# Row maxima of a first attention layer from 32-row products of two heads in two row groups, and four instead of five key tiles summed on GpSimd

## The reference

```python
tokens = x.reshape(B, C, N).transpose(0, 2, 1)
qkv = (tokens @ w_proj + b_proj).reshape(B, N, NUM_HEADS, 3 * HEAD_DIM)
q, k, v = jnp.split(qkv, 3, axis=-1)
attn = jnp.einsum('bihd,bjhd->bijh', q, k) * SCALE
attn = jax.nn.softmax(attn, axis=2)
res = jnp.einsum('bijh,bjhd->bihd', attn, v).reshape(B, N, NUM_HEADS * HEAD_DIM)
out = res @ w_out + b_out + tokens
```

## Time and profile before

| | |
|---|---|
| median of 3 runs | 2839.39 us |
| profiled execution | 2838.16 us |
| its span, first to last instruction | 2836.4 us |
| TensorE matmul busy | 2652.5 us, 94% |
| VectorE busy | 1983.4 us, 70% |
| ScalarE busy | 1286.8 us, 45% |
| GpSimd busy | 698.3 us, 25% |
| granted TensorE clock, mean | 0.981 |

### The profile page before, as it was taken

The page is one execution under the profiler, slowest core; times in us unless marked ns, Lnnn a source line. Parts: engine busy times, 40 slices in busy tenths (PEclk is TensorE's granted clock), DMA queues, the critical chain, the costliest instruction groups (busy, mean ns, idle before and its releaser), DMA issues.

```text
span 2836.4 us, 44487 instructions
## 1 busy us (share of the span) xinstructions
PE 2652.5 (94%) x15932; PEld 1852.8 (65%) x15932; DVE 1983.4 (70%) x2297; ACT 1286.8 (45%) x1874; POOL 698.3 (25%) x444
## 2 busy tenths in 40 slices
PE   5899999999999999999999999999999999999994
PEld 4457775577656776567755777557775577656772
DVE  2665777666976768766786677766787666876666
ACT  2463435533365434644346343563435534364334
POOL 0440025300372014600236002540035300361011
PEclk7899999999999999999999999999999999999997
DMA  5300023000410005000050002300032000500016
GB/s 127 71 1 16 12 65 77 17 1 12 105 38 17 1 12 112 31 17 1 30 124 2 17 12 51 91 12 5 12 73 69 17 1 12 112 31 1 1 62 275
DMA packets 46238, 123.51 MB, mean 44 GB/s; under 512 B 9905, under 2 KB 21425, under 8 KB 42417
## 3 DMA queue, kind: packets, MB, share of 16 engines
q1 hardware_dynamic: 46000, 120.36, 15.9%
HBM read 41.96 MB, written 23.86 MB: 23 GB/s over the span
## 4 chain that ended last, share of the span: by engine, by line
PE 71%; issue 9%; DVE 6%; ACT 4%; SPq 4%; POOL 3%; DMA 2%; DVEq 0%; ACTq 0%; POOLq 0%
PE tile L1542 21%; PE pv L1542 11%; PE pv L1666 8%; PE tile L1628 7%; PE tile L1656 6%; PE tile L1801 4%; PE tile L1692 4%; SPq L582 3%; PE pv L1656 2%; PE tile L1823 2%; PE tile L1852 2%; DMA stack<-qk_r 1%; ACT p L854 1%; POOL qk_r L687 1%; PE tile L1720 1%
## 5 line engine op out<-in xcount | busy, mean ns | idle before, releaser
L1123 DVE TENSOR_REDUCE small<-tile 128x1 f32<-128x1024 f32 x512 | 600.0, 1216 | 130.8 <-PE tile L1628 128.2
L854 ACT ACTIVATE p<-tile 128x512 f32<-128x512 f32 (+1 forms) x632 | 405.2, 692 | 239.2 <-PE tile L1656 214.4
L745 POOL TENSOR_TENSOR row_sum<-act 128x256 f32<-128x256 f32 x32 | 41.6, 1318 | 1475.8 <-DVE act L1316 1475.8
L1542 PE MATMUL tile<-qk_r 128*128 128x512 f32 x1536 | 378.0, 395 | 0.0
L1628 PE MATMUL tile<-stack 96*128 96x512 f32 x1024 | 344.7, 436 | 19.9 <-DMA stack<-qk_r 14.9
L715 POOL TENSOR_TENSOR acc<-acc,p 128x1024 f32<-128x1024 f32 x144 | 339.2, 2385 | 4.1 <-ACT p L854 3.9
L1542 PEld LDWEIGHTS tile<-qk_r 128*128 128x128 f32 x1536 | 287.4, 188 | 66.2 <-issue 7.7
L1321 DVE TENSOR_TENSOR pl<-p,ph 128x1024 fp32r<-128x1024 f32 x128 | 158.2, 1236 | 220.8 <-ACT p L936 220.8
L1628 PEld LDWEIGHTS tile<-stack 96*128 96x128 f32 x1024 | 178.7, 192 | 188.3 <-issue 118.9
L1656 PE MATMUL tile<-stack 112*128 112x512 f32 x760 | 269.6, 420 | 24.9 <-ACT p L854 18.4
L1666 PE MATMUL pv<-p,v 128*32 128x512 f32 x2048 | 273.1, 610 | 1.4 <-ACT p L854 1.4
(11 more groups left out here) (286 smaller groups left out, 4507.2 us busy)
## 6 DMA issues: line engine op xcount, KB each, us to landing
stack<-qk_r SPq DMA_DIRECT2D x192, 256.0 KB, 5.0
x_in<-in_x_dram SPq DMA_DIRECT2D x8, 1024.0 KB, 5.0
act<-in_x_dram SPq DMA_DIRECT2D x8, 1024.0 KB, 4.9
x_scratch<-act SPq DMA_DIRECT2D x7, 1024.0 KB, 4.0
z_scratch<-act SPq DMA_DIRECT2D x7, 1024.0 KB, 3.9
stack<-ones SPq DMA_DIRECT2D x16, 256.0 KB, 4.7
w3f<-w3f_scratch SPq DMA_DIRECT2D x8, 512.0 KB, 3.3
fin_rest<-z_scratch SPq DMA_DIRECT2D x3, 1024.0 KB, 8.5
```

What stands on the lines that cost most here:

```text
L854: sc.activation(p0[:, jt % DEPTH, pair, first:first + len(heads) * HALF], tile_wait(batch, "st0", *u, jt, k), ACT.Exp, scale=float(D) ** - ...
L1123: ve.tensor_reduce(maxima[:, h * NT + it:h * NT + it + 1], t, X, ALU.max).then_inc(vector_done, vector.one("max0", g, h, it))
L1542: ins = mm(out, lhs[a][kt_], rhs[c][kt_], start=first and kt_ == 0 and m == 0, stop=last and kt_ == n - 1 and m == 2)
```

## The change

- `s0(g, h, it)` is for a pair of heads and one half of the keys: of h, `h // 2` is the pair and `h % 2` the half. Its two matmuls contract over 32 rows, the high parts alone, and lie in the two row groups of the two heads. The second head's result goes to the second bank. In the head (the first unit) they read `qk_r`, elsewhere `stack`. The number of matmuls and of s0 stays.
- `max0` reduces the tile to two maxima, one a head; the two halves of the keys go to `maxima` and `maxima2`, and `max_both` takes the larger.
- The parts of each head are stacked in another order (`ROWS`), so that the product of the high parts of head h lies in row group h. Head 3 has its maxima in rows 64 to 96 (32 rows, of which the first 16 are zeroed by `mask8`), and its st0 contracts over 128 rows.
- VectorE spreads the maxima of heads 0 and 3, ScalarE those of 1 and 2. `key_ones` is two DMAs a group. `neg_copy` and `mh` are gone; `neg_hi` writes to its place at once.
- In the head the s0 wait for no DMA; the first unit's st0 of key tile 0 wait for the stacks.
- SUMMED is 4 in place of 5: in units 0, 1 and 2 GpSimd sums key tiles 0 to 3, den0 takes 4 to 7.

```diff
-K0 = IMAX + NMAX
+ROWS = ((0, 1, 2), (1, 0, 2), (2, 0, 1), (3, 0, 1))
+IMAX_OF = (96, 96, 96, 64)
+NMAX_OF = (NMAX, NMAX, NMAX, 2 * NMAX)
+K0_OF = (IMAX + NMAX, IMAX + NMAX, IMAX + NMAX, P)
+VECTOR_ROWS = (0, 3)
+SCALAR_ROWS = slice(1, 3)
-SUMMED = 5
+SUMMED = 4
...
             def key_ones(g):
-                sp.dma_start(stack[IMAX:K0, g, 1].rearrange("p h (a n) -> p (h a) n", n=P).bitcast(F32),
-                             ones[0:NMAX, :].rearrange("p (a n) -> p a n", a=1)
-                             .broadcast_to((NMAX, G * N // P, P))).then_inc(key_ones_in[g], 16)
+                for rows, n, heads in ((IMAX_OF[0], NMAX_OF[0], slice(0, G - 1)), (IMAX_OF[-1], NMAX_OF[-1], slice(G - 1, G))):
+                    k = heads.stop - heads.start
+                    sp.dma_start(stack[rows:rows + n, g, 1, heads].rearrange("p h (a n) -> p (h a) n", n=P).bitcast(F32),
+                                 ones[0:n, :].rearrange("p (a n) -> p a n", a=1)
+                                 .broadcast_to((n, k * N // P, P))).then_inc(key_ones_in[g], 16)
...
-                    for k, pair in enumerate((slice(0, 4, 2), slice(0, 4, 3), slice(1, 3))):
+                    for k, pair in zip(ROWS[h], (slice(0, 4, 2), slice(0, 4, 3), slice(1, 3))):
...
                 def max0(g, h, it):
                     t = tile_wait("s0", g, h, it)
-                    ve.tensor_reduce(maxima[:, h * NT + it:h * NT + it + 1], t, X, ALU.max
+                    pair, part = divmod(h, 2)
+                    dst = (maxima, maxima2)[part].rearrange("p (h t) -> p h t", h=G)[:, 2 * pair:2 * pair + 2, it]
+                    ve.tensor_reduce(dst, t.rearrange("p (q n) -> p q n", q=2), X, ALU.max
...
+                    if heads == G:
+                        m2 = maxima2.rearrange("p (h t) -> p h t", h=heads)[:, :, ts]
+                        TT(m3, m3, m2, ALU.max).then_inc(vector_done, vector.one("max_both", *key))
+                        own("max_both", *key)
...
                 def s0(g, h, it):
-                    if it == 0 or it == HT:
-                        pe.wait_ge(stacked[g][h], 48 * batch_of(("s0", g, h, it)) + 48)
+                    pair, part = divmod(h, 2)
+                    ahead = of_head(("s0", g, h, it))
+                    if ahead and (h, it) == (0, 0):
+                        scalar_wait("qk0_hi", 1, 0)
+                    elif not ahead and it % HT == 0 and part == 0:
+                        for q in range(2):
+                            pe.wait_ge(stacked[g][2 * pair + q], 48 * batch + 48)
                     o = free("s0", g, h, it)
-                    for s in halves:
-                        ins = mm(o[:, s], stack[0:IMAX, g, 0, h, it * P:(it + 1) * P], stack[0:IMAX, g, 1, h, s],
-                                 start=True, stop=True)
+                    for q in range(2):
+                        rows = slice(D * (2 * pair + q), D * (2 * pair + q) + D)
+                        i = slice(it * P, (it + 1) * P)
+                        queries, keys = ((qk_r[rows, g, t, 0, n] for t, n in ((0, i), (1, halves[part]))) if ahead else
+                                         (stack[rows, g, t, 2 * pair + q, n] for t, n in ((0, i), (1, halves[part]))))
+                        ins = mm(o[:, halves[q]], queries, keys, start=True, stop=True)
...
                 def st0(g, half, jt, k):
...
+                    if (g, half) == UNITS[0] and jt == 0:
+                        for h in heads:
+                            pe.wait_ge(stacked[g][h], 48 * batch + 48)
...
-                        ins = mm(o[:, halves[q]], stack[0:K0, g, 1, h, jt * P:(jt + 1) * P],
-                                 stack[0:K0, g, 0, h, halves[half]], start=True, stop=True)
+                        ins = mm(o[:, halves[q]], stack[0:K0_OF[h], g, 1, h, jt * P:(jt + 1) * P],
+                                 stack[0:K0_OF[h], g, 0, h, halves[half]], start=True, stop=True)
```

More of the change, by code:

```diff
@@ L182, in front @@
         s += [("max", layer, it) for it in range(NT)]
-        s += [("neg_hi", layer), ("neg_copy", layer), ("neg_lo", layer), ("max_in", layer), ("v_lo", layer, 1)]
+        s += [("neg_hi", layer), ("neg_lo", layer), ("max_in", layer), ("v_lo", layer, 1)]
         return s
@@ L208, in vector_steps @@
         s += [("max0", *rows_of(UNITS[0], k))]
-    s += [(n, *UNITS[0]) for n in ("neg_hi", "neg_copy", "neg_lo")]
-    s += [("max_rows", *UNITS[0], h) for h in range(G // 2)]
+    s += [(n, *UNITS[0]) for n in ("max_both", "neg_hi", "neg_lo")]
+    s += [("max_rows", *UNITS[0], h) for h in VECTOR_ROWS]
     for u in UNITS:
@@ L221, in vector_steps @@
         if following:
-            s += [(n, *following) for n in ("neg_hi", "neg_copy", "neg_lo")]
-            s += [("max_rows", *following, h) for h in range(G // 2)]
+            s += [(n, *following) for n in ("max_both", "neg_hi", "neg_lo")]
+            s += [("max_rows", *following, h) for h in VECTOR_ROWS]
     s += [("stat", 1, 0, ct) for ct in range(CT)]
@@ L245, in of_head @@
         return name[1] == 0 and name[3] < HT
-    if kind in ("m0", "neg_hi", "neg_copy", "neg_lo", "max_rows", "max_cols"):
+    if kind in ("m0", "max_both", "neg_hi", "neg_lo", "max_rows", "max_cols"):
         return unit == UNITS[0]
@@ L253, in of_first_layer @@
     kind = name[0]
-    if kind in ("neg_hi", "neg_copy", "neg_lo"):
+    if kind in ("neg_hi", "neg_lo"):
         return len(name) == 3
     return kind in ("stat", "out0", "s0", "st0", "m0", "pv0", "den0", "ex0", "exp0", "max_cols", "pv0_out", "res_hi",
-                    "max0", "max_rows", "add0", "rec0", "rows0", "res", "res_lo", "x1") and (kind, name[1]) not in (
+                    "max0", "max_both", "max_rows", "add0", "rec0", "rows0", "res", "res_lo", "x1") and (kind, name[1]) not in (
                         ("stat", 2), ("stat", 3))
@@ L1162, in max_rows @@
                     t = tile_wait("m0", g, half)
-                    for h in range(G // 2):
-                        spread(stack[IMAX:K0, g, 0, h, half * HALF:(half + 1) * HALF], t[0:NMAX, h * P:(h + 1) * P], ts
+                    for k, h in enumerate(VECTOR_ROWS):
+                        rows = slice(IMAX_OF[h], IMAX_OF[h] + NMAX_OF[h])
+                        spread(stack[rows, g, 0, h, half * HALF:(half + 1) * HALF], t[0:NMAX_OF[h], k * P:(k + 1) * P],
+                               mask8[0:NMAX_OF[h], NMAX_OF[h] // NMAX - 1, ts]
                                ).then_inc(vector_done, vector.one("max_rows", g, half, h))
@@ L1297, in layer_front @@
                     t = tile_wait("m", layer)
-                    spread(max_in[0:NMAX, :], t[0:NMAX, 0:P], slice(0, NT)).then_inc(vector_done, vector.one("max_in", layer))
+                    spread(max_in[0:NMAX, :], t[0:NMAX, 0:P], mask8[0:NMAX, 0]).then_inc(vector_done, vector.one("max_in", layer))
                     v_lo(layer, 1)
```

46 lines of the change are left out of this document (24 added, 22 removed).

## The result

The kernel after took 2905.94 us, the median of its runs, against 2839.26 for the kernel before in the same runs: a ratio of 1.0222, interval [1.0184, 1.026]. (One of its four runs took 3318.0 us with a granted clock of 0.741; the ratio leaves it out, and the median of the other three is 2900.69 us.) Forecast were 2862 us and a range of 2806 to 2888: the sign was right, the size was not. The profiled execution took 2911.2 us, its span is 2909.0, and the mean granted clock is 0.960 for 0.981 before.

The account below looks back on a forecast made before the run. The prediction took TensorE's order of instructions and mode changes as the bound; its terms, +1.32 - 1.30 + 0.60 + 2.73 - 0.50 = +2.85 us per sample, +23 for 8, on 2839.4 gave 2862 us, range 2806 to 2888.

Parts of the forecast that it names:

- (a): s0 as two 32-row matmuls in two row groups: +1.32, -1.30 and +0.60 us per sample across the units' key tiles.
- x: TensorE's cost per change of row mode, bounded 0 to 0.16 us, taken as 0.16.
- l: Lag of a pair's second matmul behind its first on TensorE, bounded 0 to 0.11 us, taken as 0.05.
- Tiles 0 to 2 of unit 0: Unit 0's first key tiles, before ScalarE's 2.76 us wait: pairs change nothing; without that cover +0.1 to +0.4 us each.
- the gate in (c): The second group's 12 DMA issues and landing, on which ScalarE's key tile 2 waits; forecast 0 to 1.19 us earlier.
- (c): Head's s0 reads qk_r, so its first wait for DMA, 1.19 us, goes: -0.50 us per sample.
- (b): GpSimd sums four key tiles, not five; den0 gets 32 more records on the path in three units: +2.73 us per sample.
- (d): Small edits, such as max_both for neg_copy and the wider spread of maxima: 0 us, hidden by other work.
- Rival 1: Entering a row mode costs nothing and pairs overlap fully: -3.6 us per sample, 2810 us; chance 0.38.
- rival 2: The two matmuls of a pair don't overlap, mode changes come on top: +10.9 us per sample, 2926 us; chance 0.08.
- rival 3: Fewer GpSimd adds relieve an unseen wait and give den0's 22 us back: 2840 us; chance 0.07 together with the rest.

Follow-up runs that it names:

- the third experiment: The kernel before with 32-row pairs only in the s0 for units 1, 2 and 3, head keeping 96 rows: 2867.83 us, ratio 1.0117.
- the first experiment: The kernel before with only SUMMED changed from 5 to 4: 2856.41 us, ratio 1.0074.
- The five matmuls: The kernel after with SUMMED = 5 and five useless full-width matmuls written before unit 0's first score tile: 2861.62 us, ratio 1.0084.

## Why the prediction was wrong

Point by point, by its own steps:

- **(a), the cost of a pair and of a change of mode: the sum right, partly by luck.** x = 0.16 was taken from the column mode and is 0.19; l was taken as 0.05 and is 0. In a middle key tile the one error is +0.1 and the other -0.1, so that 3.19 us came out as forecast. For units 1 and 2 that left +0.3 each with pairs alone, where (a)'s terms come to +0.22 (four middle key tiles +0.44, key tiles 0 and 7 -0.52, 1 and 2 +0.30).
- **(a), "Tiles 0 to 2 of unit 0 lie ahead of the gate in (c) ...: nothing either way": this is the step that failed**, together with the costing of the rest of unit 0 as if it were unit 1. For the sum of the work the step was right: in samples of the third experiment without a fall unit 0 is 28.7 and 28.9 us with pairs, for 28.6. But the sentence treats a wait as a cover that makes work free. The measured price of pairs there is 35 us a run, through the clock, and the prediction has no term for the clock. It took the 1.00 of the earlier trace rows from one sample's head and unit 1. The trace of the kernel before had the warning in unit 0 of three other samples; this is the fourth sample's, the stretch and then the whole unit:

```profile
1123.40:1126.80 3.40, 3.40 (x13) 1.52 (x6) 0.64 (x1) 0.98 (x3) 3.40 (x2) 0.50 0.00 0
1112.50:1142.60 30.10, 27.45 (x133) 13.47 (x131) 23.04 (x25) 18.11 (x37) 18.78 (x8) 0.94 0.44 116
```

The last sentence of the prediction names a falling clock, but in the head, where it kept 1.00 in all samples but the first.
- **(b), den0: right.** 0.91 us forecast, 0.87 measured; in the chain of the kernel after den0 holds 4.50 for 3.63 (forecast 4.54):

```profile
494.19 4.50 PE tile L1726 x160
```

- **(c), the head: right in sign, too small.** -0.50 was taken out of 0 to -1.19; it is -1.4 a sample, outside those ends, and -7 up to the first `m0`. The 12 DMAs of the second group are issued from 424.30 on, 34.8 us after the sample's first step (389.5), for 35.9 (427.38 less 391.5): 1.1 us earlier. I had let VectorE's wait of 0.35 be what is late next and had counted one such wait. It has a second one of 0.40 some 3 us later, also for TensorE, and both went. The two kernels' timelines; before:

```profile
407.26 1.16 DVE L1416 TENSOR_TENSOR qv<-pv,b3row 128x1024 f32<-128x1024 f32 x1
...
414.72 0.16 DVE L1431 COPY pairs<-pv 128x4 f32<-128x4 f32 x1 [0.40 <-PE pv L1913]
```

After, the same two instructions are 6.52 us apart in place of 7.46, without a wait:

```profile
405.33 1.16 DVE L1436 TENSOR_TENSOR qv<-pv,b3row 128x1024 f32<-128x1024 f32 x1
...
411.85 0.15 DVE L1451 COPY pairs<-pv 128x4 f32<-128x4 f32 x1
```

- **(d), small edits at 0: wrong by what they moved, not by what they do.** The 32 bytes that `mask8` grew by cost 1.1 us in each sample's layers 1 and 2, 9 us. The instructions added moved the program, and TensorE began to stop behind group norm: 16 to 18 us. No row of the profile before could price either; a range could have.
- **Rival 1** (2810 us, x and l at 0) is out by the pitch of 3.19; **rival 2** (no overlap) by the 0.50 of a pair, though its sign and size look close to the result; **rival 3** by the first experiment.

With unit 0 as it was and at undisturbed places, the change would have come to some 2836 - 14 (head) + 5 (units 1 and 2) + 21 (den0) = 2848 us, an estimate from the parts, inside the range. On the same base the ratio of 1.0222 puts the kernel after at 2899 us; the other 51 us are the clock in unit 0, the program's place and the tensors' place.

What stays open: why unit 0 falls 3 to 5 us after `m0` in some samples and 10 to 13 in others, and how much of it is the lighter matmul and how much the wait, 1.04 us for 0.77, that a faster pair leaves in front of the first st0. The five matmuls left that wait as it was and took away the falls behind it, which speaks for the matmul, but no run separates the two. Nor does one separate what of a pair counts, its 32 rows or the half of the time that it takes: no kernel here has a single 32-row matmul in place of a pair.

## What to carry to other kernels

Cutting a matmul's rows to a third cost far more here than it saved where TensorE also waits: look through all samples for stretches at the low clock before a stage is priced, price each stage with a wait in it once at the full clock and once at half, and put light matmuls first where the engine doesn't wait. When a change of several parts is slower, take it apart before giving it up: here one part alone, the head, was worth 0.5%, and the same pairs cost at most 5 us in two units and 35 us in a third. Compare stages that the change does not touch: 27 us of this loss stood in them, from 32 bytes and from moved instructions. And look in the trace whether a filler stands in the wait that it was written for.

## What was not expected of the hardware

- **The low clock can last without a gap.** TensorE at 20.50 busy of 20.50 us was granted 0.50 (1.2 GHz), and at 27.30 of 27.30 in another kernel, with a 32-row pair in every few matmuls; what went before was a wait. The kernel before has waits at the same places (0.77 us and 1.4 to 1.7) and 3.4 us stretches behind the second, three in the seven later samples (10 us in all, for 109 in the kernel after). In units 1 and 2 the same pairs without such waits keep 1.00 (2.4 GHz). The Trainium skill (TensorE: Matmul & The Clock Gate, section HAM oscillation — how this bites in real kernels) names idle gaps as what takes the clock. The trace agrees in so far as the stretches start behind waits; but these waits are of 0.6 to 2.4 us, shorter than the gaps of which the section speaks, and no gap shows in the 27.30 us through which the clock stayed low.
- **32 bytes of a tensor's place** change the pace of some full-width matmuls: 163.29 us busy against 164.31 for the same 762 matmuls.
- **A change of row mode** costs 0.19 us each way, a change of column mode 0.16, and a pair in two row groups costs the time of one matmul.
